# Two attention layers with relative positions, from a stage per step to one block with the next projection inside

## The reference, cut to what matters

```python
def layer0(x):                        # DIM 192, 12 heads of 16, windows of 14 x 14
    xn = ln(x, ln1_w, ln1_b)
    xw = windows(pad(xn))             # 4 windows per image, 196 keys each
    q, k, v = split(xw @ qkv_w + qkv_b)
    attn = q * scale @ k.T + rel_h[..., :, None] + rel_w[..., None, :]
    x = x + unwindow(softmax(attn) @ v @ proj_w + proj_b)
    h = gelu(ln(x, ln2_w, ln2_b) @ fc1_w + fc1_b)
    return x + h @ fc2_w + fc2_b

def layer1(x):                        # one window per image, 256 keys
    q, k, v = split(x @ w_qkv + b_qkv)
    attn = q * scale @ k.T + rel_h + rel_w
    return softmax(attn) @ v @ w_proj + b_proj

x = layer0(x)
x = x + layer1(group_norm(x))         # 32 groups over image and channels
```

## Time and profile before

| | us |
|---|---|
| median of 3 runs | 1480.7 |
| lowest and highest | 1478.15 and 1488.42 |
| the profiled execution | 1474.58 |
| its span | 1472.4 |
| TensorE's mean granted clock in it | 0.829 |
| PE, DVE, ACT busy | 1127.6, 581.0, 390.0 |

### The profile page before, as it was taken

The page is one execution under the profiler, slowest core; times in us unless marked ns, Lnnn a source line. Parts: engine busy times, 40 slices in busy tenths (PEclk is TensorE's granted clock), DMA queues, the critical chain, the costliest instruction groups (busy, mean ns, idle before and its releaser), DMA issues. The chain is left out here.

```text
span 1472.4 us, 27845 instructions
## 1 busy us (share of the span) xinstructions
PE 1127.6 (77%) x10374; PEld 781.0 (53%) x10375; DVE 581.0 (39%) x1709; ACT 390.0 (26%) x932; POOL 88.9 (6%) x130
## 2 busy tenths in 40 slices
PE   2779796976687779897968519994697897558993
PEld 1647464843554547574736407773373573436772
DVE  5143112323232527473857612222573374421223
ACT  2103210320141145352524103331251252112220
POOL 2000010000000000000000040003100000040004
PEclk9769785977697799897979659997797998768997
DMA  7000000002000000007400141111920000021113
GB/s 190 3 2 3 1 2 2 3 1 83 4 1 1 3 1 1 1 2 160 162 0 1 33 110 43 48 48 46 206 74 1 0 2 1 1 72 46 48 48 102
DMA packets 32150, 57.28 MB, mean 39 GB/s; under 512 B 3557, under 2 KB 28870, under 8 KB 31018
## 3 DMA queue, kind: packets, MB, share of 16 engines
q1 hardware_dynamic: 28856, 48.44, 12.2%
q0 software_dynamic: 3072, 6.30, 1.5%
q10 hardware_dynamic: 114, 1.04, 0.3%
HBM read 41.80 MB, written 13.86 MB: 38 GB/s over the span
## 5 line engine op out<-in xcount | busy, mean ns | idle before, releaser
L1612 PE MATMUL banks<-gu,sxT 96*128 x496 | 177.8, 503 | 0.8 <-ACT sxT L1647 0.6
L215 PE MATMUL banks<-xT,weights 96*96 96x512 f32 (+3 forms) x288 | 148.5, 675 | 9.4 <-ACT xT L423 8.8
L1013 ACT ACTIVATE work<-banks,nmax 128x128 f32<-128x128 f32 (+1 forms) x288 | 105.6, 418 | 108.0 <-DVE nmax L1052 107.8
L1673 DVE TENSOR_TENSOR h<-sg,banks 128x384 f32<-128x384 f32 x62 | 34.4, 554 | 236.4 <-ACT sg L1655 236.4
L1612 PEld LDWEIGHTS banks<-gu,sxT 96*128 96x128 f32 x496 | 92.7, 197 | 54.6 <-issue 7.6
L1052 DVE TENSOR_REDUCE nmax<-banks 128x2 f32<-128x256 f32 (+1 forms) x144 | 80.2, 557 | 64.4 <-PE banks L957 62.3
L215 PEld LDWEIGHTS banks<-xT,weights 96*96 96x96 f32 (+3 forms) x288 | 55.1, 196 | 92.7 <-issue 73.9
L932 PE MATMUL banks<-K,Q 96*128 96x128 f32 (+1 forms) x384 | 86.1, 351 | 11.1 <-PEq L88 11.1
L696 ACT ACTIVATE work<-banks 98x1024 f32<-98x1024 f32 (+1 forms) x48 | 49.2, 1024 | 144.8 <-PE banks L620 144.8
L754 DVE TENSOR_REDUCE nmax<-banks 98x4 f32<-98x784 f32 (+1 forms) x48 | 52.6, 1100 | 74.7 <-PE banks L594 54.2
L1061 DVE COPY work<-banks 128x256 f32<-128x256 f32 (+1 forms) x144 | 79.2, 550 | 0.4
(11 more groups left out here) (235 smaller groups left out, 1661.4 us busy)
## 6 DMA issues: line engine op xcount, KB each, us to landing
gu<-in_L2f_gu SPq DMA_DIRECT2D x1, 6912.0 KB, 37.0
xin<-slots_in SPq DMA_DIRECT2D x62, 96.0 KB, 1.9
slots_out<-y SPq DMA_DIRECT2D x62, 96.0 KB
gu<-in_L3f_gu SPq DMA_DIRECT2D x1, 5184.0 KB, 31.4
dn<-in_L2f_dn SPq DMA_DIRECT2D x1, 4608.0 KB, 47.9
slots_in<-zeros SPq DMA_DIRECT2D x1, 2976.0 KB, 10.8
dn<-in_L3f_dn SPq DMA_DIRECT2D x1, 2592.0 KB, 37.3
gu<-in_L2f_gu SPq DMA_DIRECT2D x1, 2304.0 KB, 13.0
```

The lines of the kernel that those rows point to most:

```text
L215: ins = nc.tensor.matmul(out, lhs(k, rows), rhs(k, rows), start=(k == 0), stop=(k == 1))
L1013: ins = nc.scalar.activation(w.Pr[0:rows, s % 3, hh, 0:lay.width(t)], S(s)[0:rows, hh, 0:lay.width(t)], ACT.Exp, bias=w.nmax[0:rows, s % 4 ...
L1612: ins = nc.tensor.matmul(banks[:, 2 + 2 * par + n, 0:EF], w.sxT[:, par, k, :], w.gu[:, bass.ds(e, 1), k, n * EF:(n + 1) * EF].rearrange("p ...
```

## The change

Both layers become one block of one stage, `convolution_layers`, with a class `Relative` that holds the former steps as methods per engine. The lists of the engines are written out: an attention is split into a late part (relative products of group g, then the scores of unit g - 1), a main part (scores of units 6 to 11 beside transposed scores of units 0 to 5), and a second half (transposed scores of units 6 to 11), which carries the turn, the queries and the keys of the next pair between its own steps. The values of the next pair follow, and in layer 0 the feed-forward of this pair. Banks are laid out anew: the next projection uses a ring of banks 0 to 3, transposed scores always banks 4 and 5. `X` is the residual itself, `R` is used for `NT` only. The queries wait for both halves of `xT`. The zeroing of `slots_in` and the constant rows of layer 1 move into the one setup. Layer 1 shares the buffers of layer 0; its keys lie in the part of layer 0's `K` that belongs to the first image.

```diff
-        for layer, windows in (("L0", True), ("L1", False)):
...
-                relative_setup(nc, env, w, windows)
-                for ip in range(IMAGES // PAIR):
-                    relative_project(nc, env, w, ip, windows)
-                    attend_relative(nc, env, w, ip, windows)
-                    if windows:
-                        feed_forward(nc, env, w, ip, False)
+            first_loads(nc, env, d, w, blob)
+            relative_setup(nc, env, w, w1)
+            convolution_layers(nc, env, w, w1)
...
+            def late(L, ip, ring_read=None):
+                for g in range(6):
+                    L.pe_relative(pe, ip, g, ring_read)
+                    if g >= 1:
+                        L.pe_scores(pe, ip, g - 1)
+                    if g == 4:
+                        L.pe_turn_max(pe, ip, 0)
+                L.pe_scores(pe, ip, 5)
+            def main(L, ip):
+                for i in range(6):
+                    L.pe_scores(pe, ip, 6 + i)
+                    if i in (0, 3):
+                        L.pe_turn_max(pe, ip, 1 + i // 3)
+                    L.pe_scores_turned(pe, ip, i)
+                    if i in (2, 4):
+                        L.pe_weigh(pe, ip, i // 2 - 1)
...
+            for L, ip, N, nip in ((L0, 0, L0, 1), (L0, 1, L1, 0), (L1, 0, L1, 1), (L1, 1, None, 0)):
+                L.pe_turn_max(pe, ip, 3)
+                L.pe_scores_turned(pe, ip, 6)
+                L.pe_weigh(pe, ip, 2)
+                if N is not None:
+                    N.pe_turn(pe, nip)
+                L.pe_scores_turned(pe, ip, 7)
+                L.pe_turn_outputs(pe, ip, 0, 0)
+                if (N, nip) == (L0, 1):
+                    L1.pe_window_tables(pe)
+                L.pe_scores_turned(pe, ip, 8)
+                L.pe_weigh(pe, ip, 3)
+                L.pe_turn_outputs(pe, ip, 0, 1)
+                if N is L1:
+                    N.pe_stats(pe, nip)
+                L.pe_scores_turned(pe, ip, 9)
+                L.pe_turn_normed(pe, ip, 0)
+                L.pe_scores_turned(pe, ip, 10)
+                L.pe_weigh(pe, ip, 4)
+                L.pe_project(pe, ip, 0)
+                if N is not None:
+                    N.pe_queries(pe, nip, 0)
+                L.pe_scores_turned(pe, ip, 11)
+                if N is not None:
+                    N.pe_queries(pe, nip, 1)
+                    N.pe_keys(pe, nip, 0)
+                L.pe_weigh(pe, ip, 5)
+                if N is not None:
+                    N.pe_keys(pe, nip, 1)
+                    N.pe_keys(pe, nip, 2)
+                L.pe_turn_outputs(pe, ip, 1, 0)
+                L.pe_turn_outputs(pe, ip, 1, 1)
...
+                L.pe_project(pe, ip, 1)
+                if N is not None:
+                    N.pe_keys(pe, nip, 5)
+                    for j in range(N.jobs):
+                        N.pe_values(pe, nip, j)
+                    if L is L0:
+                        F.pe(pe, ip, (N.v_out, N.jobs * (nip + 1)))
+                    late(N, nip, (F.added, PT * (ip + 1)) if L is L0 else None)
+                    main(N, nip)
```

More of the change, by code:

```diff
@@ L263, in _, with relative_setup @@
             dve.wait_ge(cleared, 4)
-def relative_setup(nc, env, w, windows):
+def relative_setup(nc, env, w, w1):
     with stage(nc, env.names) as (block, sem):
-        loaded, win_made, steps, filled = w.loaded, sem("win_made"), sem("steps"), sem("filled")
+        loaded, steps, filled = w.loaded, sem("steps"), sem("filled")
         @block.sync
@@ L317, in _ @@
             chain = Chain(dve, steps)
-            if windows:
-                normalise(nc, chain, env.ahead_s, env.ahead, env.X[:, 0:PT, :], 1e-5, True)
+            normalise(nc, chain, env.ahead_s, env.ahead, env.X[:, 0:PT, :], 1e-5, True)
             dve.wait_ge(loaded, 16 * len(w.loads))
-            if not windows:
-                dve.wait_ge(win_made, 1)
-                for n in range(2):
-                    chain.free(nc.vector.tensor_copy(w.win[:, n, :, :].rearrange("p a b -> p (a b)"),
-                                                     env.banks[0:CH, n, 0:TOKENS]))
-                chain.wait()
@@ L349, in relative_project, with window_tables_steps, convolution_layers @@
+def window_tables_steps(nc, chain, w):
+    for s in range(2):
+        chain.free(nc.vector.tensor_copy(w.bd[:, 0, :, s, 16:32], w.qslot[:, None, s, :].to_broadcast([CH, SIDE, HD])))
+        yield
+        chain.free(nc.vector.memset(w.bd[:, 1, :, s, 16:32], 0.0))
+        yield
+        for n in range(2):
+            chain.free(nc.vector.tensor_scalar(w.bd[:, n, :, s, 0:16], w.win[:, n, :, :], w.odd[:, s:s + 1], None, ALU.mult))
+            yield
+def convolution_layers(nc, env, w0, w1):
     with stage(nc, env.names) as (block, sem):
@@ L368, in _ @@
+        @block.sync
+        def _(sp):
+            for L in (L0, L1):
+                for ip in range(2):
+                    for b in range(4):
+                        L.sp_max(sp, ip, b)
+        @block.gpsimd
+        def _(pool):
+            for ip in range(2):
+                L0.pool_windows(pool, ip)
         @block.vector
@@ new lines, in late_and_main @@
+            def late_and_main(L, ip, extra, per_step):
+                L.dve_relative(dve, ip, 1)
+                L.dve_maxima(dve, ip, 0)
+                L.dve_maxima(dve, ip, 1)
+                L.dve_relative(dve, ip, 3)
+                L.dve_maxima(dve, ip, 2)
+                L.dve_maxima(dve, ip, 3)
+                L.dve_turned_max(dve, ip, 0)
+                L.dve_relative(dve, ip, 5)
+                L.dve_maxima(dve, ip, 4)
+                L.dve_maxima(dve, ip, 5)
+                for i in range(6):
+                    L.dve_maxima(dve, ip, 6 + i)
+                    if i in (0, 3):
+                        L.dve_turned_max(dve, ip, 1 + i // 3)
+                    for _ in range(per_step):
+                        next(extra, None)
+                for _ in extra:
+                    pass
@@ L816, in _ @@
             chain.wait()
-            for t in range(2):
-                divide(1, t)
-            residual(1)
+            dve.wait_ge(L1.added, 4)
 class Layout:
```

1085 lines of the change are left out of this document (613 added, 472 removed).

## The result

| | before | after |
|---|---|---|
| median of 4 runs each, us | 1482.53 | 1404.2 |
| lowest and highest | 1478.15 and 1488.42 | 1393.87 and 1411.3 |
| the profiled execution, its span | 1474.58, 1472.4 | 1411.3, 1409.5 |
| mean granted clock in it | 0.829 | 0.841 |

The ratio of the times is 0.946, with a 95% interval of 0.939 to 0.954: 78 us faster between the medians, 63.3 between the two profiled executions. Before going into steps, one thing about the numbers: after's four runs differ by 17 us, and they stand in the order of their clock (1411.3 at 0.841, 1407.4 at 0.844, 1401.0 at 0.849, 1393.9 at 0.853). The profiled one is the slowest.

What follows compares the result with a forecast made beforehand. The prediction took PE's idle time (stage boundaries, waits for maxima, handovers ending attentions), with the clock on top, as the bound. Four stretches changing -19.8, -33.2, -12.0, +4.0 us, plus 0.7, gave -60.3 off 1480.7: 1420, range 1378 to 1452.

Steps and rivals of the forecast that it cites:

- the second rival: In the three filled halves, VectorE's and ScalarE's in-order lists stall PE: 31 us come back, 1451 us; chance 0.19.
- its last rival: PE was already the bound, only boundaries go: about -46, 1435 us; counted as upper part of the forecast's 0.62.
- The late part: Relative products with scores of units 0 to 5, at half clock: 34.5 us in layer 0, 32.4 in layer 1.
- The first rival: Full clock in the late parts of both layers: -65 us in all, 1355 us; chance 0.13.
- Main parts: Scores 6 to 11 beside transposed scores 0 to 5: 24.2 us, layer 1 17.6, each with 2.5 for the clock.
- Filled halves: Second halves of attentions with the next projection inside: 49.4 us in the first pair, 42.7 second, 36.6 third.
- the third rival: Small passes hold clock 0.50 through main parts and filled halves: +165, about 1585 us; chance 0.06, including anything as bad.
- Feed-forward: In layer 0, barrier and the norm's 3.03 us wait go: 27.5 us against 31.88 before.
- End of layer 1: Last half, with no projection to fill it: 22.9 us; fourth stretch 72.9 against 68.9, +4.0.
- The sum: Over four stretches between relative products: -19.8, -33.2, -12.0 and +4.0, with +0.7 for queries; total -60.3 us.
- The start: Ahead of the first relative product, the first pair's queries wait for both halves of the input: +0.7 us.

Runs made afterwards that it cites:

- e2_projection_behind: Changed kernel with the next pair's turn, statistics, queries and keys moved behind the last output projection; median 1433.18 us, ratio 0.967 to the kernel before.
- e5_wide_products: Changed kernel with scores behind all six groups of relative products, each product there writing 64 columns in place of 32; one run, 1429.55 us.
- e7_half_count: Changed kernel with scores behind all six groups, and only every other relative product, 64 columns each; one run, 1389.49 us.
- e4_double_scores: Changed kernel with the near score products of units 0 to 5 issued twice into the same place; median 1401.0 us, ratio 0.947 to the kernel before.
- a1_again: The changed kernel unaltered, timed again for its spread; median 1393.25 us, ratio 0.942 to the kernel before.
- a2_again: The changed kernel unaltered, timed once more on another chip; median 1413.84 us over six runs, ratio 0.950 to the kernel before.

## Why the prediction was right, and where its sizes were off

*Direction and mechanism: right in the main.* PE's idle time was the gain. No barrier wait is left between the marks, PE is busy in 92% (forecast: above 85%), and no wait for a VectorE result inside a filled half comes near 2 us, so the second rival fell. Both halves of the change carry: undoing the interleaving costs 35 to 45 us, undoing the filling 40. The whole is 85.6 on that chip (1478.88 - 1393.25); if the two add up, which no run shows, 1 to 11 us stay for the barriers and the second setup by themselves, where the view of waits has 15.4 us of PE's waits at barriers. The prediction had priced those boundaries alone, as its last rival, at 46, with two norm chains in it; `e2_projection_behind` shows that without the filling the chain comes back as PE's wait, wherever the barrier is. No run took the barriers alone away, so their own price stays open. One cause in the prediction was half right: of the 16.9 us that PE is idle in the second layer's first projection, 8.7 are "issue" gaps in its relative products, not the group norm.

*The late part: the step that was mis-sized.* Forecast 34.5 and 32.4 us from the first relative product to scores 6; measured 31.0 and 28.5 in layer 0, and in layer 1 27.3 (323.80 to 351.1, half of the two units' 3.79 us behind 349.21) and 28.3. That is 3.5 + 6.0 + 5.1 + 4.1 = 19 us, more than the whole difference of the sum. The false sentence is "relative products without a gap fell to 0.50", with the conclusion that their 19.4 us are TensorE time at a low clock. The row that was quoted for it says otherwise: PE busy 11.85 of 21.20 us. Of the 9.35 idle, 1.9 stand at the barrier behind, and 7.5 are five gaps of 1.2 to 1.8 us inside the products, which the view of waits lists:

```profile
PE banks L512 <- issue: 7.5, 5, 1.8
```

They are PE's wait for its next block of 256 instruction records. `e5_wide_products` put twice the columns into the same time, `e7_half_count` made it little more than half with half the records. The interleaving closes most of these gaps, and the term had carried them over: 28.7 us of them before and 8.3 after are 20.4 us, which is about the 19 by which the late parts came out shorter. So "group plus unit" is not 3.2 + 2.36 = 5.6 us but 4.38.

*The first rival was mis-sized by the same error.* It said -65 for a full clock in the late parts. `e4_double_scores` had 0.80 to 0.89 there and took 126.8 us for the four, with more work, `a1_again` half clock and 122.6. With its supply at 4.0 us a group and unit and PE at 4.38, a faster array has by estimate less than 0.4 us a group to give. The rival did not occur (0.52 to 0.59 in the late parts), as forecast, but it would not have been worth 1355. The rule weighed there, from the Trainium skill ("TensorE: Matmul & The Clock Gate", the section on oscillation), asks for PE without long idle gaps. The prediction held against it that the groups follow one another, which rows 2 don't show; but between 66.2 and 83.0 after has PE busy in 16.80 of 16.80 us at a clock of 0.50, so here that was not enough.

*Main parts.* 21.9 and 23.2 us against 24.2: the 2.5 charged for the clock to rise was a little high. In layer 1, main part and last half together take 39.5 against 40.5.

*Filled halves.* The second took 41.6 (forecast 42.7); the third with the main part before it 53.7 (17.6 + 36.6 = 54.2). The first took 63.3 in the profiled execution and 50.0 in `a1_again`, forecast 49.4. The work was counted right, and so was the place of the waits (`banks L522 <- ACT work L627` sums to 9.1 us in 18 places, none over 0.9). What was missing is a small form of the third rival: the clock can fall for 17 to 30 us inside a filled half, in some executions, and then costs 11 to 16 us of that stretch. The length that was to show this rival, a filled half of layer 0 above 60 us, did occur in the profiled execution, at a clock of 0.76 and in one half only. The one kernel's times from 1392 to 1416 go with their mean clock. Of the 19 us between the profiles of after and `a1_again`, 16 lie in the first stretch; of the 21 between `a2_again` and `a1_again`, 11.5 lie there and 9.3 in the untouched layers behind. The fall isn't tied to the 0.89 us wait; what decides it is open.

*Feed-forward.* 26.8 and 29.05 against 27.5. As forecast, the input scaling of the second step is what PE waits for. The second is longer because the layer-1 values are only 2.7 us of cover for the norm (timeline of PE in after):

```profile
296.96 1.05 PE L795 MATMUL banks<-small,xn 128*96 128x128 f32 x8 [2.20 <-DVEq L1064]
```

The prediction named the values as the norm's cover, and did not redo the sum for the pair in which they shrink from 10.6 to 2.7. `e2_projection_behind` has the same wait, 2.21.

*End of layer 1.* The last half has the forecast handovers (timeline of PE in after), yet the fourth stretch did not become longer than before, because the late part in front of it was 4 us shorter than sized:

```profile
466.33 1.06 PE L541 MATMUL banks<-work,V 128*17 128x256 f32 x16 [1.12 <-ACT work L627]
...
471.01 1.57 PE L215 MATMUL banks<-weights,OT 96*128 96x192 f32 x8 [0.68 <-ACT OT L645]
```

*The sum.* Late parts -19, mains and the other halves -6, first half +14, feed-forwards +1: the 414.2 against 424.0. That the sum came so close is in part luck, because the two largest errors have opposite signs. In `a1_again`, where the first half lost no clock, it is 397.3, 27 below the forecast. The start took 3.9 us where 0.7 was charged: 0.8 is a later turn (28.21 for 27.44), 0.8 more a wait for the scaled input, 1.6 the queries and keys (16.3 us for 14.6), and 0.7 a wait for the last value's copy. Behind the last projection another 4 us were not charged. There the next stage's barrier ends a wait of 4.71 us, 3.83 before, in `a1_again` too, where this part is 0.7 longer than before; the other 3 belong to the one execution.

## What to carry to other kernels

Before calling a stretch of small matmuls bound by the clock, read PE's busy time against its length in the stage view, then the waits marked "issue", then the instruction queue in the view of DMA. Here PE was busy for 11.85 of 21.2 us, with 7.5 us of such waits in five gaps and five instruction packets: instructions, not columns, were short. Such a stretch is the place for work with few and long instructions, and it takes some of it nearly free, until the gaps are closed. Behind that point more filling gained nothing here, and the values cost 18.4 us in place of 10.6, since the clock was at half there. When a dependent chain is hidden by work that changes in size from pass to pass, redo the sum for the smallest.

## What the runs showed of the hardware

- PE's instructions came in packets of 16,384 bytes on a DMA queue of their own, one for 256 records (128 matmuls and 128 weight loads). Small products alone used up a packet in 1.95 us and got the next after 3.46 to 4.0, so PE stood for 1.2 to 2.1 us each time, and the mean was 13.5 ns a record at best.
- 64 columns in place of 32 took the same time so (PE busy 9.46 and then 15.87 of 17.0 us). With scores between the groups, which closed the gaps, a group took 2.02 us with 32 columns and 3.57 with 64, at half clock; with 32 columns at full clock it took 2.0.
- The granted clock of one kernel is not the same from run to run. The same 6248 records of PE between the marks took 364.7 us of busy time at a mean clock of 0.85 and 381.2 at 0.81, and PE was busy in 29.8 of 30 us in which most of the clock was at 1.2 GHz.
- Doubling eight matmul records per unit, 48 more of PE's records in a late part, brought its clock from between 0.52 and 0.59 to between 0.80 and 0.89, and the four late parts from 122.6 to 126.8 us.
